# The last layer norm before the router, folded into the router's weights

## The reference

```
x = x + L0_attn(layernorm(x))            # gated linear attention, 16 heads
x = x + L0_xattn(layernorm(x), ctx, ...) # mLSTM cross attention, 8 heads of 32, per batch
x = x + L0_ffn(layernorm(x), ...)        # mixture of 8 experts

def L0_ffn(hidden_states, ...):
    normed = _layernorm(hidden_states, rn_g, rn_b)
    logits = einsum('bld,ed->ble', normed, router_w) + router_b
    top_w, top_idx = top_k(logits, 2);  top_w = softmax(top_w)
    for e in range(8):
        h = gelu(_layernorm(hidden_states, ln_g[e], ln_b[e]) @ w1[e] + b1[e]) @ w2[e] + b2[e]
        out = out + combine[..., e:e+1] * h
```

## Time and profile before

| | |
|---|---|
| median of three timed runs | 762.63 us (761.96 to 763.38) |
| profiled execution, its own time | 764.05 us |
| span of the profiled execution | 762.3 us |
| TensorE matmul busy | 724.8 us (95%) |
| VectorE busy | 397.4 us (52%) |
| ScalarE busy | 361.1 us (47%) |
| GpSimd busy | 439.1 us (58%) |
| mean granted clock of TensorE | 0.983 of 2.4 GHz |

### The profile page before, as it was taken

The page is one execution under the profiler, slowest core; times in us unless marked ns, Lnnn a source line. Parts: engine busy times, 40 slices in busy tenths (PEclk is TensorE's granted clock), DMA queues, the critical chain, the costliest instruction groups (busy, mean ns, idle before and its releaser), DMA issues.

```text
span 762.3 us, 17120 instructions
## 1 busy us (share of the span) xinstructions
PE 724.8 (95%) x5856; PEld 654.2 (86%) x5857; DVE 397.4 (52%) x1000; ACT 361.1 (47%) x936; POOL 439.1 (58%) x510
## 2 busy tenths in 40 slices
PE   7999999979999999888999879999999999999995
PEld 5677777759999999887999757999999999999994
DVE  2566777675756443333999994333333433333331
ACT  1444434444766444335999535534444344344341
POOL 6577777776777777774776401344444444544543
PEclk7999999999999999998999999999999999999999
DMA  9334444443333363662998995112212222122121
GB/s 295 98 104 132 140 133 126 136 131 97 94 97 106 107 211 98 146 200 68 263 266 209 310 365 184 29 34 34 41 34 34 36 39 34 34 34 41 34 34 22
DMA packets 75812, 88.29 MB, mean 116 GB/s; under 512 B 11952, under 2 KB 66032, under 8 KB 75632
## 3 DMA queue, kind: packets, MB, share of 16 engines
q0 software_dynamic: 19824, 43.93, 23.3%
q1 hardware_dynamic: 52256, 40.11, 18.2%
q10 hardware_dynamic: 3680, 3.54, 1.4%
HBM read 75.82 MB, written 11.73 MB: 115 GB/s over the span
## 4 chain that ended last, share of the span: by engine, by line
PE 41%; issue 26%; POOL 20%; DVE 7%; DMA 4%; ACT 2%; POOLq 1%; DVEq 0%; ACTq 0%
PE ps L2050 10%; POOL out L1691 8%; POOL G L1670 5%; PE ps L1031 5%; PE ps L485 4%; POOL G L332 4%; PE ps L1287 2%; PE ps L552 2%; PE ps L478 2%; PE ps L526 2%; DMA G<-in_rpe,hopi 2%; DMA out<-G,slots 2%; PE ps L450 1%; PE ps L576 1%; PE ps L1289 1%
## 5 line engine op out<-in xcount | busy, mean ns | idle before, releaser
L332 POOL DMA_INDIRECT G<-in_rpe,hopi x193 | 188.7, 978 | 63.4 <-issue 51.5
L1809 ACT ACTIVATE G<-ps,U 128x128 f32<-128x128 f32 x312 | 84.7, 383 | 161.4 <-PE ps L1744 161.4
L1744 PEld LDWEIGHTS ps<-G,QT 128*128 128x128 f32 x1248 | 145.2, 192 | 2.0
L1744 PE MATMUL ps<-G,QT 128*128 128x128 f32 x1248 | 145.5, 275 | 0.0
L1752 PE MATMUL ps<-G 128*128 x624 | 141.2, 379 | 1.4 <-DVE G L1986 1.4
L1752 PEld LDWEIGHTS ps<-G 128*128 128x128 f32 x624 | 115.5, 190 | 15.8 <-issue 1.7
L2050 PE MATMUL ps<-U,PET 128*128 128x128 f32 (+3 forms) x768 | 102.2, 278 | 0.0
L2050 PEld LDWEIGHTS ps<-U,PET 128*128 128x128 f32 x768 | 95.9, 196 | 0.1
L979 DVE COPY PET<-ps 128x512 f32<-128x512 f32 x64 | 44.2, 690 | 90.0 <-PE ps L1031 88.4
L1691 POOL DMA_INDIRECT out<-G,slots x39 | 68.9, 1768 | 23.8 <-issue 23.8
L2093 ACT ACTIVATE PET<-ps 128x512 f32<-128x512 f32 (+1 forms) x63 | 37.4, 594 | 89.8 <-PE ps L1031 86.3
(11 more groups left out here) (241 smaller groups left out, 1255.2 us busy)
## 6 DMA issues: line engine op xcount, KB each, us to landing
G<-run_max SPq DMA_DIRECT2D x16, 512.0 KB, 8.1
U<-in_w SPq DMA_DIRECT2D x16, 512.0 KB, 8.0
G<-in_w SPq DMA_DIRECT2D x8, 1024.0 KB, 11.5
G<-in_rpe,hopi POOLq DMA_INDIRECT x193, 2.9
U<-in_ctx SPq DMA_DIRECT2D x8, 256.0 KB, 2.8
tokens_kept<-X SPq DMA_DIRECT2D x8, 256.0 KB, 2.4
X<-tokens_kept SPq DMA_DIRECT2D x1, 2048.0 KB, 9.9
hidden_rows<-QT ACTq DMA_DIRECT2D x8, 256.0 KB, 7.1
```

The source lines that it names most:

```text
L332: pool.indirect_dma_start(out=dst, out_offset=None, in_=rpe_d, in_offset=bass.IndirectOffsetOnAxis(ap=hopi[:, n:n + 1], axis=0)) \
L1744: mm = pe.matmul(bank(1 + 2 * u + c // 4, 4, P)[:, c % 4], w1c[u][:, k, c], hT[u][:, k, :], start=(k == 0), stop=(k == KC - 1))
L1809: ins = nc.scalar.activation(gel[u][:, c, :], bank(1 + 2 * u + c // 4, 4, P)[:, c % 4], ACT.Gelu, bias=b1c[u][:, c:c + 1])
```

## The change

Instead of normalised rows TensorE now turns the raw rows of `X`, as soon as they are final, and the layer norm is applied to the logits. For a row x with mean m and inverse deviation s, (x - m) s W = s (x W - m sum(W)); with the weights centred, W' = W - sum(W) / 256, the term with m vanishes and the logits are s (x W'). So:

- `router_sums` on TensorE sums the weights' columns (two more small matmuls beside the two of the bias), and `router_centred` on VectorE subtracts the mean from `rwp`.
- `turn_rows(b)` replaces `turn_hidden(b)` and waits for `x2_r` and no longer for `hid_r`. Batches 0 to 3 are turned before the last `values`.
- `scaled_logits` replaces `add_bias`: two instructions for each batch, which multiply by the inverse deviation and add the bias.
- The stored rows are still the normalised ones. ScalarE makes them now (`rows(b)`: Identity with scale s and bias -m s), and GpSimd makes the bias -m s (`negated_shift`).
- The order of the streams is rewritten around that. The last batch's moments move in between the `top_two` calls.

```diff
-            def third_rows():
-                b = 2
+            def negated_shift(b):
                 pool.wait_ge(frs_r, b + 1)
-                pool.wait_ge(hid_r, b)
                 for c in range(2):
-                    ins = nc.gpsimd.tensor_scalar(hid[b][:, c, :], X[:, 2 * b + c, :], fmv[b][:, c, 0:1],
-                                                  frs[b][:, c:c + 1], ALU.subtract, ALU.mult)
-                ins.then_inc(hid_r, 1)
+                    ins = nc.gpsimd.tensor_scalar(fnm[b][:, c:c + 1], fmv[b][:, c, 0:1], frs[b][:, c:c + 1], -1.0,
+                                                  ALU.mult, ALU.mult)
+                ins.then_inc(fnm_r, 1)
...
-            third_rows()
+            for b in range(3):
+                negated_shift(b)
             pool.wait_ge(fresh, 1)
             weighted(B - 1)
             residual(B - 1)
+            for b in range(3, B):
+                negated_shift(b)
...
-            def turn_hidden(b):
-                pe.wait_ge(hid_r, b + 1)
+            def turn_rows(b):
+                pe.wait_ge(x2_r, b + 1)
                 if b >= NZ:
                     pe.wait_ge(hT_cp, b - NZ + 1)
                 for k in range(KC):
                     for c in range(2):
-                        mm = pe.transpose(bank(b % NZ, KC, 2, P)[:, k, c], hid[b][:, c, k * P:(k + 1) * P], ident)
+                        mm = pe.transpose(bank(b % NZ, KC, 2, P)[:, k, c], X[:, 2 * b + c, k * P:(k + 1) * P], ident)
                 mm.then_inc(hT_full, 1)
+
+            def router_sums():
+                pe.wait_ge(f_w, 1)
+                for i, lhs in enumerate((rnbb, None)):
+                    for k in range(KC):
+                        mm = pe.matmul(bank(6, 2, E)[:, i], ones if lhs is None else lhs[:, k, :],
+                                       rwp[:, k, :] if lhs is None else rwT[:, k, :], start=(k == 0), stop=(k == KC - 1))
+                mm.then_inc(f_rb, 1)
...
-                if b == 1:
+                if b == 0:
...
                 if u == NUNIT - 1:
                     pe.wait_ge(mk_r, B)
-                    pe.wait_ge(x2_r, 1)
-                    keep_going(1, KEYS)
+                    pe.wait_ge(v1_r, B)
+                    router_sums()
+                    pe.wait_ge(add_r, NUNIT)
+                    for b in range(NZ):
+                        turn_rows(b)
                 values(u)
 
...
             logits(0)
-            turn_hidden(2)
             logits(1)
-            logits(2)
             pe.wait_ge(fresh, 1)
-            turn_hidden(3)
-            for b in range(4, B + 1):
-                if b < B:
-                    turn_hidden(b)
-                logits(b - 1)
+            for b in range(NZ, B):
+                turn_rows(b)
+                logits(b - 2)
+            logits(B - 2)
+            logits(B - 1)
...
+            def rows(b):
+                act.wait_ge(fnm_r, b + 1)
+                for c in range(2):
+                    ins = nc.scalar.activation(hid[b][:, c, :], X[:, 2 * b + c, :], ACT.Identity, scale=frs[b][:, c:c + 1],
+                                               bias=fnm[b][:, c:c + 1])
+                ins.then_inc(hid_r, 1)
...
+            for b in range(NZ):
+                copy_turned(b)
             row_inv_std(0)
             row_inv_std(1)
             evict(B - 1)
             row_inv_std(2)
-            copy_turned(0)
+            row_inv_std(3)
             inv_std(B - 1)
+            row_inv_std(4)
+            copy_turned(4)
+            rows(0)
+            row_inv_std(5)
+            copy_turned(5)
             store_rows(0)
-            row_inv_std(3)
-            copy_turned(1)
+            act.wait_ge(fresh, 1)
+            copy_turned(6)
+            row_inv_std(6)
+            rows(1)
             store_rows(1)
-            row_inv_std(4)
+            copy_turned(7)
+            rows(2)
+            row_inv_std(7)
             for b in range(2, B):
-                copy_turned(b)
+                if b > 2:
+                    rows(b)
                 store_rows(b)
-                if 3 <= b < 5:
-                    row_inv_std(b + 2)
-                if b == 5:
-                    act.wait_ge(fresh, 1)
-                    row_inv_std(B - 1)
+            act.wait_ge(hid_r, B)
             act.dma_start(z_dram[B * S:B * S + P], hid[B - 1][:, 0]).then_inc(z_st[1], 16)
...
-            def hidden_rows(b):
+            def router_centred():
+                dve.wait_ge(f_rb, 1)
+                nc.vector.tensor_tensor(rbb, bank(6, 2, E)[:, 0], rbb, ALU.add)
+                nc.vector.scalar_tensor_tensor(rwp, bank(6, 2, E)[:, 1].unsqueeze(1).to_broadcast([P, KC, E]), -1.0 / D, rwp,
+                                               ALU.mult, ALU.add).then_inc(f_rs, 1)
+
+            def scaled_logits(b):
                 dve.wait_ge(frs_r, b + 1)
+                dve.wait_ge(lg_full, b + 1)
+                spacer()
                 for c in range(2):
-                    ins = nc.vector.tensor_scalar(hid[b][:, c, :], X[:, 2 * b + c, :], fmv[b][:, c, 0:1],
-                                                  frs[b][:, c:c + 1], ALU.subtract, ALU.mult)
-                ins.then_inc(hid_r, 1)
-
-            def add_bias(b):
-                dve.wait_ge(lg_full, b + 1)
-                nc.vector.tensor_tensor(LG[:, 2 * b:2 * b + 2, :], bank(7 - b % 2, 2, NRP, E)[:, :, 0, :],
-                                        rbb.unsqueeze(1).to_broadcast([P, 2, E]), ALU.add).then_inc(lg_cp, 1)
+                    ins = nc.vector.scalar_tensor_tensor(LG[:, 2 * b + c, :], bank(7 - b % 2, 2, NRP, E)[:, c, 0, :],
+                                                         frs[b][:, c:c + 1], rbb, ALU.mult, ALU.add)
+                ins.then_inc(lg_cp, 1)
...
+            router_centred()
...
             spread(B - 1)
+            dve.wait_ge(f_rs, 1)
+            scaled_logits(0)
             mean_var(4)
             scale(B - 1)
-            dve.wait_ge(f_rb, 1)
-            nc.vector.tensor_tensor(rbb, bank(6, E), rbb, ALU.add).then_inc(f_rs, 1)
-            dve.wait_ge(f_rs, 1)
-            add_bias(0)
-            dve.wait_ge(hid_r, 3)
-            hidden_rows(3)
-            hidden_rows(4)
+            scaled_logits(1)
             moments(5)
-            add_bias(1)
+            scaled_logits(2)
             mean_var(5)
+            scaled_logits(3)
+            dve.wait_ge(fresh, 1)
...
                 top_two(0, 2)
-                add_bias(4)
+                scaled_logits(5)
                 top_two(2, 4)
-                add_bias(5)
+                moments(B - 1)
+                scaled_logits(6)
+                mean_var(B - 1)
                 top_two(4, 6)
-                add_bias(6)
                 link(top_two(6, 7))
                 link(one_hot_experts(0, T - 2))
-                add_bias(7)
+                scaled_logits(7)
```

More of the change, by code:

```diff
@@ L1086, in build @@
         frs = [cw(2) for _ in range(B)]
+        fnm = [cw(2) for _ in range(B)]
         rwp, LG = cw(KC, E), cw(T, E)
@@ L1093, in build @@
         fresh = sem("fresh")
+        fnm_r = sem("fnm_r")
         nrm_r, nsq_r = sem("m_nrm_r"), sem("m_nsq_r")
@@ L1337, in mlstm_tensor @@
                     pe.wait_ge(mk_r, B)
-                    pe.wait_ge(x2_r, 1)
-                    keep_going(1, KEYS)
-                values(u)
-            pe.wait_ge(mk_r, B)
-            pe.wait_ge(v1_r, B)
-            pe.wait_ge(add_r, NUNIT)
-            pe.wait_ge(f_w, 1)
-            for k in range(KC):
-                mm = pe.matmul(bank(6, E), rnbb[:, k, :], rwT[:, k, :], start=(k == 0), stop=(k == KC - 1))
-            mm.then_inc(f_rb, 1)
-            turn_hidden(0)
-            turn_hidden(1)
+                    pe.wait_ge(v1_r, B)
[3 more added lines that the diff above has]
+                        turn_rows(b)
+                values(u)
             logits(0)
-            turn_hidden(2)
             logits(1)
-            logits(2)
             pe.wait_ge(fresh, 1)
-            turn_hidden(3)
-            for b in range(4, B + 1):
-                if b < B:
-                    turn_hidden(b)
-                logits(b - 1)
+            for b in range(NZ, B):
[3 more added lines that the diff above has]
+            logits(B - 1)
         def mlstm_scalar(act, at=None):
@@ L1556, in mlstm_vector @@
             mean_var(1)
-            hidden_rows(0)
             moments(3)
             mean_var(2)
-            hidden_rows(1)
+            moments(4)
             mean_var(3)
-            moments(4)
             spread(B - 1)
+            dve.wait_ge(f_rs, 1)
+            scaled_logits(0)
             mean_var(4)
             scale(B - 1)
-            dve.wait_ge(f_rb, 1)
-            nc.vector.tensor_tensor(rbb, bank(6, E), rbb, ALU.add).then_inc(f_rs, 1)
-            dve.wait_ge(f_rs, 1)
-            add_bias(0)
-            dve.wait_ge(hid_r, 3)
-            hidden_rows(3)
-            hidden_rows(4)
+            scaled_logits(1)
```

(20 more changed lines are left out.)

## The result

Eight timed runs of the changed kernel have a median of 769.28 us (766.20 to 771.01), eight of the kernel before on the same chip 762.52 us (761.38 to 764.54): a ratio of 1.009, 95% interval 1.0072 to 1.0107, about 7 us slower. The forecast was 760.6 us. The profiled execution took 769.50 us with a span of 767.7, against 764.05 and 762.3.

What follows compares the result with a forecast made beforehand. Bound between 429 and 464 us: VectorE's routing, then TensorE's fill. Slots were forecast 2.4 us earlier, held by the stores' landing; less 0.4 for copy and gather overlapping, 2.0 off 762.63 gives 760.6 us, range 758.5 to 764.4.

Steps and rivals of the forecast that it cites:

- VectorE, last pick: VectorE's routing: the last routing count picked at 447.1 us, 4.3 us earlier than before.
- the small waits: VectorE waiting for the logits of batches 3 to 5 from TensorE: about 0.9 us together.
- ScalarE, mis-sized: ScalarE's row passes and stores: 1.05 us a batch, last store at 449.4, small exponential 449.5, losing 1.6 of 4.3 us.
- The stores' landing: Store queue before the fill: the last store issued at 449.4 takes 7.5 us, so rows land at 456.9.
- the slack: Between the stores' landing and ScalarE's need of it for the one-hots: 3.5 us in the kernel before.
- TensorE's clock, the step that failed: Rival: clock falls behind a fill waiting for stored rows, fillers double to 10.7 us; +3.4 us, 766.0, chance 0.13.
- the wait before the fill grows: TensorE ahead of the fill: wait from 2.2 to about 4 us; three fillers take 5.1 instead of 4.27, hidden.
- the whole 2.4 us forecast for the cast: Cast of the slots behind the fill: at 461.9 instead of 464.3 us, a gain of 2.4 us.
- signs of being wrong: VectorE waiting over 2 us for ScalarE or TensorE before 447, cast behind 464, or clock below 1.00 after 460.
- the late case: Rival: stores land at 460.3, slots at 465.2; +0.9 to +1.9 us, 763.5 to 764.5; chance 0.20.
- twelve fillers: TensorE's warm-keeping matmuls between the fill and the first transposes: 5.36 us, doubling to 10.7 if the clock falls.

Runs made afterwards that it cites:

- fillers 3 and 8: Changed kernel with three warm-keeping matmuls added behind the last logits and eight instead of three ahead of the fill: ratio 1.0034.
- the late exponential and 7 fillers: Kernel before with 13 chained ScalarE copies ahead of the small exponential and seven instead of three warm-keeping matmuls ahead of the fill: ratio 1.0033.
- mix: Changed kernel, stored rows 0, 1, 2, 4, 6 on VectorE and 3, 5, 7 on ScalarE, stores issued once rows are ready: 759.38 us, 0.9965.
- split: Changed kernel, stored rows 0, 6, 7 on GpSimd, exponential behind store 5, two warm-keeping matmuls behind the last logits, four ahead of the fill: 1.0040.

## Why the prediction was wrong

In order of the prediction's steps, in us behind the origin (forecast from 428.41, measured from 426.47):

- **VectorE, last pick:** forecast 18.7, measured 18.5. Right, with the small waits too (0.77, 0.45 and 0.29).
- **ScalarE, mis-sized:** a batch was put at 1.05 us (two passes at 0.40 and 0.25 for the store) and took 1.54. The row taken was the 0.40 between two exponentials that don't depend on each other, 0.50 us long at most; the passes took 0.59 each. A store of rows just made waits for the second pass to end (1.10 for the pair) and then takes 0.37 to issue, a length that the earlier trace rows show. So the last store left at 23.5, not 21.0, and the exponential behind it came at 24.05, not 21.1. With the 23.77 of before, ScalarE gave back all 4.5 us and 0.3 more.
- **The stores' landing:** forecast 28.5, measured 29.6, from late middle stores and not from the last one's latency. It was in the slack either way. The page of the Trainium skill that the prediction weighed, "DMA: Bandwidth & Descriptors", section "Latency and other measured facts", has about 2 us of fixed cost; from the last issue to the landing 6.1 us went by here, in which the queue still moved 0.96 MB.
- **TensorE's clock, the step that failed.** The prediction had the clock as a rival, priced at +3.4 us and 0.13, and placed it behind the fill, if the fill stood waiting for stored rows. It saw that "the wait before the fill grows" and that the fillers there may run at 1.2 GHz, "hidden, since the planes are not ready before". The fillers' time was hidden (5.24 us, 5.1 forecast); what was not is that TensorE had nothing to do between them and the fill (2.32 us), and that all but the first records of the fill and most of the six fillers behind it then ran at half clock: 5.97 and 2.33 us more. The fill had been taken at its old 7.34 us. The kernel before without its fillers shows this price with nothing else changed.

What the change would be worth at full clock is read from the changed kernel with fillers 3 and 8: its fill begins at 27.60, its inputs end where they did (34.1), and the cast comes at 36.01, 0.1 us later than before the change. So two errors add up: ScalarE's mis-sized term took the whole 2.4 us forecast for the cast (33.5), since the fill's inputs hang on the exponential, and the clock cost 5.1 us more at the cast and 2.3 behind it.

Two of the prediction's own signs of being wrong came: the cast at 467.61, behind 464, and a clock of 0.50 after 460. Slips in its sums change nothing: 452.9 and 2 us of fixed cost give 454.9 and not 454.7, 458.49 less 2.7 is 455.8, and the late case ends at 764.5, not 764.4. Its "twelve fillers" are six matmuls of two records each; their 5.36 us were read rightly.

What stays open is how much idleness brings the clock down. 1.51 and 2.32 us directly ahead of the fill did, 0.99 behind 7 us of fillers did not, and in two kernels several waits of 0.2 to 0.7 us did. It isn't the length alone either: the 2.3 us of idle time ahead of the routing's counts were followed by half clock in the kernel before and by full clock in the one with the late exponential and 7 fillers, and the instructions up to there were the same on TensorE.

## What to carry to other kernels

When a change makes one engine earlier and another later, look at TensorE between the two: an idle gap of 1.5 to 3.3 us ahead of 32 short matmuls cost 6 us on them, more than any input was late. In these runs fillers paid when they reached to the start of the real work or within 1 us of it, and cost time when they went beyond it. When work moves to the engine that also issues the stores, count its pass, the wait for its own result and the issue as one sum, and look at when the middle stores leave: the queue moved 0.25 MB where it had moved 0.67 in the same 4 us, and the rest was still ahead of the last store.

## What the runs showed of the hardware that was not expected

- Taking three matmuls away from the kernel before, at a place where TensorE had nothing else to do, made it 1.0% slower (1.0098).
- In the changed kernel the granted clock came back to full at 451.5 us, stayed there through the idle stretch from 451.7 to 454.0, and fell near 455, while the fill ran: in this trace the level follows what the engine did earlier, not what it does.
- Two Identity passes over 256 columns on ScalarE, with scale and bias from a tile, took 1.10 us to the end of the second, against 0.70 to 0.73 for most pairs of the same work on VectorE and 2.42 on GpSimd.
- The last store's time to landing went roughly with the bytes that its queue still had to move, its own included: 5.4 us for 0.78 MB (mix), 6.1 for 0.96 (changed), 8.2 for 1.11 (before) and 8.0 for 1.3 (split).
